# Six slots instead of four in the two load rings of the down projection

## The reference

```python
x = layernorm(x + attention(x))            # 24 heads of 64, causal, three tiers
h = silu(x @ w_gate) * (x @ w_up)          # 2048 -> 8192
h = keep_2_largest_of_4(h)                 # by |h|, in groups of 4 features
x = layernorm(x + h @ w_down)              # 8192 -> 2048, the stage of the change
```

## Time and profile before

| what | time |
|---|---|
| median of 2 runs | 6259.35 us (6024.2 and 6494.49) |
| the profiled execution | 6016.93 us |
| its span, core 4, first to last instruction | 6015.4 us |
| the eight cores' spans | 5941.4 to 6015.4 us |
| projections | 0 to about 1090 us |
| attention, output projection, first layernorm | to about 2825 us |
| gate and up, first half; down, first half | to about 3741; 4294 us |
| gate and up, second half; down, second half | to about 5352; 5898 us |
| last layernorm | to 6015 us |
| TensorE busy; granted clock | 79% of the span; 0.90 |

### The profile page before, as it was taken

One profiled execution on the slowest core, in us unless ns is written; L12 is line 12 of the kernel. 1 busy time (PEld: TensorE's weight loads), 2 busy tenths in 40 slices (PEclk: granted clock), 3 DMA queues, 4 the chain that ended last, 5 costly groups with the idle time before them and its releaser, 6 DMA issues.

```text
span 6015.4 us, 61352 instructions; the slowest of 8 cores (5941.4 to 6015.4 us)
## 1 busy us (share of the span) xinstructions
PE 4761.7 (79%) x20075; PEld 1834.5 (30%) x20400; DVE 1839.9 (31%) x2803; ACT 1151.1 (19%) x1301; POOL 437.2 (7%) x800
## 2 busy tenths in 40 slices
PE   0588989666758858885999997888893999978884
PEld 0233334111111212221444443333340444433331
DVE  0122122434432232223445444000155354420004
ACT  0000000526718818880000000000000000000000
POOL 0000000000000000000000000222100000012220
PEclk9999999777878878887999998999995999999996
DMA  9433234232141122112555554988642454558883
GB/s 150 72 61 61 50 64 93 69 104 50 43 119 54 50 102 71 57 36 77 91 98 98 90 97 93 188 178 182 137 96 74 84 97 93 98 120 188 173 187 96
DMA packets 360621, 592.61 MB, mean 99 GB/s; under 512 B 85504, under 2 KB 208576, under 8 KB 357056
## 3 DMA queue, kind: packets, MB, share of 16 engines
q0 software_dynamic: 155968, 260.75, 28.7%
q1 hardware_dynamic: 204352, 327.92, 17.7%
HBM read 767.26 MB, written 88.28 MB: 142 GB/s over the span
## 4 chain that ended last, share of the span: by engine, by line
PE 52%; DMA 17%; DVE 14%; ACT 7%; issue 7%; another core or an unknown queue 4%; DVEq 0%; ACTq 0%; SPq 0%; POOLq 0%; POOL 0%
PE ps L744 15%; PE ps L754 15%; DMA ar<-wd 9%; PE ps L871 7%; DMA vspill<-ar 5%; ACT ar L540 5%; DVE ar L552 4%; PE ps L348 4%; PE ps L571 2%; PE ps L517 2%; DMA ar<-wospill 2%; PE ps L441 2%; PE ps L982 1%; PE ps L679 1%
## 5 line engine op out<-in xcount | busy, mean ns | idle before, releaser
L744 PE MATMUL ps<-ar 128*128 128x512 bf16 x4014 | 1203.7, 380 | 70.7 <-DMA ar<-wg 33.6
L754 PE MATMUL ps<-ar 128*128 128x512 bf16 x4013 | 1203.3, 380 | 6.5 <-DMA ar<-wu 2.0
L871 PE MATMUL ps<-ar 128*128 128x512 bf16 x4014 | 944.7, 388 | 209.7 <-DMA ar<-wd 132.6
L540 ACT ACTIVATE ar<-ps 128x1024 bf16<-128x1024 f32 x960 | 893.6, 1091 | 193.3 <-PE ps L525 186.2
L571 PE MATMUL ps<-ar 128*65 128x512 bf16 x1920 | 633.7, 418 | 39.7 <-DVE ar L552 38.0
L871 PEld LDWEIGHTS ps<-ar 128*128 128x128 bf16 x4096 | 393.3, 99 | 761.1 <-issue 353.5
L744 PEld LDWEIGHTS ps<-ar 128*128 128x128 bf16 x4096 | 401.3, 98 | 552.7 <-issue 71.8
L774 ACT ACTIVATE ar<-ps 128x1024 bf16<-128x1024 f32 x128 | 131.1, 1024 | 2196.4 <-PE ps L744 1573.6
L754 PEld LDWEIGHTS ps<-ar 128*128 128x128 bf16 x4096 | 401.4, 98 | 488.2 <-issue 7.1
L517 PE MATMUL ps<-ar 64*128 64x512 bf16 x960 | 424.4, 463 | 131.0 <-DVE ar L1086 75.2
L552 DVE TENSOR_TENSOR ar<-ar 128x512 bf16<-128x512 bf16 x768 | 312.8, 425 | 636.8 <-ACT ar L540 594.4
(11 more groups left out here) (103 smaller groups left out, 2632.0 us busy)
## 6 DMA issues: line engine op xcount, KB each, us to landing
ar<-hspill SPq DMA_DIRECT2D x512, 256.0 KB, 4.8
ar<-wg POOLq DMA_DIRECT2D x128, 512.0 KB, 6.2
ar<-wu POOLq DMA_DIRECT2D x128, 512.0 KB, 8.8
ar<-wd POOLq DMA_DIRECT2D x512, 128.0 KB, 5.1
ar<-wospill SPq DMA_DIRECT2D x72, 512.0 KB, 3.5
hspill<-ar SPq DMA_DIRECT2D x128, 256.0 KB, 6.7
ar<-xT POOLq DMA_DIRECT2D x8, 2048.0 KB, 17.8
ar<-xTo POOLq DMA_DIRECT2D x8, 2048.0 KB, 15.4
```

Of the source, the lines that this page charges most:

```text
L540: lambda e, b0=b0, eap=eap: e.activation(eap, ps[:, b0 * 512:(b0 + 2) * 512], AF.Exp, scale=0.125),
L744: lambda e, bb=bb, th=th, kc=kc, s=s, wgs=wgs: e.matmul(bank(bb + th), wgs[:, kc * 128:(kc + 1) * 128], x1[:, kc * 2048 + s * 512: kc * 20 ...
L754: lambda e, bb=bb, th=th, kc=kc, s=s, wus=wus: e.matmul(bank(bb + 2 + th), wus[:, kc * 128:(kc + 1) * 128], x1[:, kc * 2048 + s * 512: kc ...
L871: lambda e, bi=bi, ft=ft, th=th, ic=ic, wst=wst, hst=hst: e.matmul(bank(bi), wst[:, ft * 128:(ft + 1) * 128], hst[:, th * 512:(th + 1) * 512],
```

## The change

Both rings of the down stage get six slots instead of four. `wdr` grows to columns 78848 to 81920 of the SBUF arena, `hst` gets its fifth and sixth slot behind that, at 81920 to 83968; its first four stay at 73728. Nothing else of the stage lies there. Four semaphores are new (wd4, wd5, hr4, hr5), and there is no new instruction.

```diff
-        hsw=[Buf() for _ in range(4)], hst=[Buf() for _ in range(4)],
-        wdr=[Buf() for _ in range(4)],
+        hsw=[Buf() for _ in range(4)], hst=[Buf() for _ in range(6)],
+        wdr=[Buf() for _ in range(6)],
...
             for ic in range(64):
-                rsl = ic % 4
+                rsl = ic % 6
                 rB = B["wdr"][rsl]
                 wst = A(78848 + rsl * 512, 512)
                 evl = dma("gpsimd", "wd%d" % rsl,
                           wst, wd[ic * 128:(ic + 1) * 128, fq * 512:(fq + 1) * 512],
                           waits=rB.wr_waits())
                 rB.note_write(evl)
-                hsl = ic % 4
+                hsl = ic % 6
                 hB = B["hst"][hsl]
-                hst = A(hst_o + hsl * 1024, 1024)
+                hst = A((hst_o + hsl * 1024) if hsl < 4 else (81920 + (hsl - 4) * 1024), 1024)
                 evhl = dma("sync", "hr%d" % hsl, hst,
                            hspill[ic, :, blk * 1024:(blk + 1) * 1024],
                            waits=hB.wr_waits() + B["hspill"].rd_waits())
```

## The result

The changed kernel takes 0.9736 of the time of the kernel before, 95% interval 0.9711 to 0.9761: 2.6% faster. Its profiled execution took 5861.2 us (span 5859.7) against 6016.9.

What follows compares the result with a forecast made beforehand. The four-slot load ring's latency was taken to bound the down stage, with the DMA engines next. Stage 1098 to 986 us saves 112, plus 1 for wu: 6017 - 113 = 5904 us, range 5820 to 6010.

Steps and rivals of the forecast that it cites:

- the forecast's own range: Whole kernel, if the DMA engines are filled at 1.85 to 1.96 us a down-stage step: 5875 to 5932 us, chance 0.45.
- TensorE binds: Rival for the down stage: matmuls set the pace, stage 910 us, kernel 5828 us; chance 0.17.
- the loop of L + 2.66 us: Down stage: four steps take matmuls 1.90, POOL issue 0.52, wd landing L and 0.24 us; 2.04 to 2.29 us a step.
- 1.906 us a step: Down stage: forecast DMA cost of one step's wd and h loads plus instruction fetches, at a share of 1.0.
- 976 us plus 10: Forecast down stages: 512 steps at the DMA engines' pace, plus 4 us at the ends and 6 for ring restarts: 986 us.
- the 13 us at 224 GB/s: Fast stretch of the earlier trace where a DMA share of 0.96 was held, cited against a limit at 0.92.
- This wait is gone as long as L stays: Down stage, six slots: by the loop alone 1.29 to 1.53 us a step, under TensorE's 1.72, if landing time L is unchanged.
- The third case: Rival: DMA engines already at their limit at share 0.92, 2.07 us a step, kernel 5983 us; chance 0.30.
- The slower case: Rival: more loads in flight make each byte dearer, 2.28 us a down-stage step, kernel 6090 us; chance 0.08.
- an allowance of 16: Down stage, if matmuls set the pace: 16 us added for landings beyond 7.84 us and the changes of `fq`.
- The changes of `fq`: Down stage: the ring restarts at slot 0 six times, four loads each waiting four steps back; 6 us, bounds 0 and 9.
- The 0.98 us for wu: End of the first down half: L754's wait for wu goes because POOL issues the next loads two steps earlier.

## Why the prediction was right, and where it was not

The time, 5861 us in the profiled execution, lies in the range of 5820 to 6010, but 43 us under the forecast of 5904 and below the forecast's own range of 5875 to 5932. The wide range held three of the four cases, so that the time lies in it speaks for none of them, and in part it is luck. Faster by over 2% had 0.37. The case that came is the one to which I gave 0.17: TensorE binds. Of the signs that I had named, the waits under 60 us and the share above 0.95 fit both cases; the two that tell them apart, landings of 7 us or more and stages of 490 us, came out at 6.3 and 470.

**What bound the kernel before.** Right, and now shown: the loop of L + 2.66 us over four slots. Five, six and eight slots give the series it calls for, and shorter landings with four slots give much of the same gain. I had read it off the wd loads alone, though; the h ring was in the same state behind them. A slip beside it: a granted clock of 0.97 is some 33 us lost, by an engine that was at 1.2 GHz for twice as long, not "some 30 us in which the engine had fallen". Nothing in the sum used it.

**The step that failed: what the DMA engines can do.** I took 1.906 us a step at a share of 1.0 as their pace, from share divided by bytes over the whole stage, and so 976 us plus 10. Measured with half of the matmuls left out: 1.775 us a step at a share of 1.04 on the core first shown, 1.70 at 1.06 on the best, and the engines may be able to do better still. So their pace was not above TensorE's 1.79 (1.72 in my sum), and the wait that I forecast never formed. Both halves of the quotient were off. First, the cost per MB fell when the queues were full. The queue lines of the changed kernel from 3748 to 4216:

```profile
q0 software_dynamic: 36211, 33.59, 53.9%
q1 hardware_dynamic: 36426, 66.31, 46.4%
```

wd costs 53.9% x 468 / 33.59 = 7.51 us per MB, much the same as the 7.57 of before, and h 46.4% x 468 / 66.31 = 3.27 instead of 3.46; a step comes to 1.84 us against my 1.90. Second, 1.0 isn't the top of the scale: the share adds up the times of packets, and 1.04 to 1.06 means that some of them overlap. The bounds that I had written down were the better guide: the 13 us at 224 GB/s are 393,216 B / 224 = 1.755 us a step, within the 1.70 to 1.79 measured. I took the mean "since the ring has to live through both" stretches, but the slow ones go with the loop's waits, which the change removes.

**The slots' own terms.** "This wait is gone as long as L stays": L rose to 6.3 us and not to 7 or more, as the forecast wanted it. The third case, a limit at a share of 0.92, is refuted by shares of 0.99 to 1.06. The slower case, in which more loads in flight make a byte dearer, is refuted in its sign: six slots cost 1.84 us a step, four 1.90.

**TensorE binds, 5828 us.** The right mechanism, its sum 910 us for stages that took 939. The floor is 918, 37 us over 881, and of these I had only the 13 for L889. Over that the changed kernel had 21 us, of which 13.7 are waits and 21 x 0.18 = 4 us restarts, against an allowance of 16.

**The small terms.** The changes of `fq` were put at 6 us and cost nothing that shows. The 0.98 us for wu went as said, and the eviction wait before L744 shrank by 1.4 us, which I hadn't said. The first matmul's wait is 28.88 us and not 28.63, so six h loads at once delay the first by 0 as taken.

**The pages.** The Trainium skill says that all DMAs run on the same 16 engines ("DMA: Bandwidth & Descriptors", section "Issuing engines are not separate DMA queues"). No run here tests that rule, and it was no argument against the change: the same loads on the same queues went from 182 to 213 GB/s, so there was rate left. By the 358 GB/s a core of the Trainium skill's HBM Reference, "Specifications (TRN2)", a step could take 1.46 us, an estimate; the shortest that these runs show is 1.70, when half of the matmuls are left out, and no run tells what the nearest limit of the loads is.

## What to carry to other kernels

When a ring of buffers waits, compute the landing time that its depth allows, (slots - 1) x step - issue, and compare it with the landing time of the trace; every ring of the step has its own, and the later landing hides the other. The DMA share of a stretch in which the ring itself makes the loads wait is no measure of what the engines can do; take the best stretch without waits, or leave out half of the compute and look. And add buffers until the longest landing fits, not the median: with these floors eight slots were worth 3 to 21 us over six in the stages, by core, too little for the ratios to tell.

## What was not expected of the hardware

The mean DMA share went above 1.0, to 1.04 at 221 GB/s and 1.06 at 231, with loads that cast for a third of their bytes, and the same kernel's loads kept a pace that differed by 5% from core to core (870 to 918 us); h loads became cheaper per MB (3.46 to 3.27 us) with more requests queued. TensorE ran its matmuls at the same pace with 221 GB/s going into SBUF and with none: 917.8 and 918.0 us on the cores shown, 918 to 922 on all eight of each.
